# Moving four evictions to ScalarE, splitting the attention products and spreading the experts' rows, in a gated-delta-rule and mixture-of-experts kernel

## The reference

```python
x = L0_attn_hidden_states
xn = _layernorm(x, axis=-1)
x = x + _L0_attn_ref(xn, ...) + _L0_ffn_ref(xn, ...)

# _L0_attn_ref: gated delta rule, 16 key heads, 32 value heads (2 per key head), width 128
#   q, k, v, z = projections of xn; a causal convolution of 4 taps and silu over q, k, v
#   q, k normalised; beta = sigmoid(b); g = -exp(A_log) * softplus(a + dt_bias)
#   per chunk of tokens: T = inverse of (I - M), M strictly lower triangular from k k^T and decays
#   scan over the chunks, per head:
v_prime = k_cumdecay_i @ state
vn = v_i - v_prime
out = q_i * exp(g_i) @ state + attn @ vn
state = state * exp(g_last) + (k_i * exp(g_last - g_i)).T @ vn
#   then out * silu(z), an rms norm, and one product with W_out

# _L0_ffn_ref: attention with 16 heads, then 16 experts of which each token takes 4
#   (w1, silu gate, w2), plus a shared expert
routed = jnp.einsum('te,teh->th', wfull, down)
return hid + (routed + shared).reshape(b, s, h)
```

## Time and profile before

| | us |
|---|---|
| median of 3 runs | 1550.68 |
| lowest, highest | 1547.57, 1552.07 |
| the profiled execution's own time | 1548.47 |
| span of the profiled execution | 1546.7 |
| busy: TensorE / its weight loads | 1514.5 / 1069.7 |
| busy: VectorE / ScalarE / GpSimd | 1104.5 / 779.7 / 442.7 |

### The profile page before, as it was taken

The page is one execution under the profiler, slowest core; times in us unless marked ns, Lnnn a source line. Parts: engine busy times, 40 slices in busy tenths (PEclk is TensorE's granted clock), DMA queues, the critical chain, the costliest instruction groups (busy, mean ns, idle before and its releaser), DMA issues.

```text
span 1546.7 us, 29212 instructions
## 1 busy us (share of the span) xinstructions
PE 1514.5 (98%) x10946; PEld 1069.7 (69%) x10946; DVE 1104.5 (71%) x2452; ACT 779.7 (50%) x1680; POOL 442.7 (29%) x280
## 2 busy tenths in 40 slices
PE   6999999999999999999999999999999999999998
PEld 4666666767656776666767767767767668668667
DVE  5364544465366335698988988988888988988966
ACT  3444445344423334664564664664664565565552
POOL 1000000006024003354444444543442541541511
PEclk9999999999999999999999999999999999999999
DMA  4342433223144434324314414414313323223211
GB/s 135 99 150 96 156 124 109 66 64 125 54 128 130 124 109 120 94 51 97 100 35 107 107 32 108 105 36 106 78 50 91 70 60 86 69 66 86 60 22 35
DMA packets 225051, 136.88 MB, mean 89 GB/s; under 512 B 160976, under 2 KB 196304, under 8 KB 224912
## 3 DMA queue, kind: packets, MB, share of 16 engines
q1 hardware_dynamic: 221840, 126.62, 30.5%
q0 software_dynamic: 3072, 8.39, 1.8%
HBM read 94.85 MB, written 35.91 MB: 85 GB/s over the span
## 4 chain that ended last, share of the span: by engine, by line
PE 90%; DVE 3%; issue 2%; POOL 2%; ACT 1%; DMA 1%; SPq 0%; POOLq 0%; DVEq 0%; ACTq 0%
PE ps L953 7%; PE ps L814 7%; PE ps L575 7%; PE ps L835 6%; PE ps L670 5%; PE ps L600 4%; PE ps L1089 4%; PE ps L704 4%; PE ps L857 3%; PE ps L590 3%; PE ps L890 3%; PE ps L742 3%; PE ps L752 3%; PE ps L1112 3%; PE ps L867 3%; PE ps L889 2%
## 5 line engine op out<-in xcount | busy, mean ns | idle before, releaser
L1440 ACT ACTIVATE vs<-ps 128x256 f32<-128x256 f32 x128 | 49.2, 384 | 255.8 <-PE ps L857 251.6
L2389 POOL TENSOR_TENSOR qg<-qT,Ebc 128x1024 f32<-128x1024 f32 x32 | 74.7, 2354 | 354.4 <-PE ps L890 329.2
L1944 DVE SCALAR_TENSOR_TENSOR cv<-ps,cw,cv 128x1022 f32<-128x1022 f32 (+2 forms) x96 | 122.8, 1280 | 18.9 <-ACT cv L1380 14.9
L1955 DVE SCALAR_TENSOR_TENSOR cv<-ps,cw,cv 128x1022 f32<-128x1022 f32 (+2 forms) x96 | 122.6, 1277 | 4.0 <-ACT cv L1412 1.6
L835 PE MATMUL ps<-xnT,gz 128*128 128x512 f32 x256 | 121.0, 596 | 0.6 <-DVE cv L1944 0.6
L953 PE MATMUL ps<-wout,xT 128*128 128x256 f32 x480 | 120.2, 392 | 1.3 <-ACT vs L1427 0.9
L575 PE MATMUL ps<-xrT,cv 128*128 128x512 f32 x256 | 117.8, 593 | 1.1 <-ACT xrT L1277 0.8
L814 PE MATMUL ps<-xnT,gv 128*128 128x512 f32 x256 | 117.6, 603 | 0.5
L2083 DVE SCALAR_TENSOR_TENSOR total<-ps,rr,total 128x256 f32<-128x256 f32 x240 | 111.6, 481 | 5.7
L1340 ACT ACTIVATE we<-ps,bias 128x128 f32<-128x128 f32 (+3 forms) x128 | 65.8, 526 | 98.2 <-DVE bias L1764 98.2
L1760 DVE TENSOR_TENSOR ps<-ps,causal_neg 128x128 f32<-128x128 f32 x128 | 37.4, 292 | 105.2 <-PE ps L600 105.2
(11 more groups left out here) (265 smaller groups left out, 3567.9 us busy)
## 6 DMA issues: line engine op xcount, KB each, us to landing
xs_dram<-zeros SPq DMA_DIRECT2D x16, 1024.0 KB, 7.6
dec<-grow_dram SPq DMA_DIRECT2D x32, 512.0 KB, 4.7
Ebc<-erow_dram SPq DMA_DIRECT2D x32, 512.0 KB, 5.0
cv<-in_wqk SPq DMA_DIRECT2D x16, 512.0 KB, 3.6
xn<-xs_dram SPq DMA_DIRECT2D x47, 128.0 KB, 2.1
ys_dram<-yg SPq DMA_DIRECT2D x47, 128.0 KB, 2.0
we<-in_we SPq DMA_DIRECT2D x16, 352.0 KB
cv<-in_wv SPq DMA_DIRECT2D x16, 256.0 KB, 3.7
```

What stands on the lines that cost most here:

```text
L1944: ins = stt(row, pair(bank)[:, :, 0:S - k], cw[:, f, i, TAPS - 1 - k:TAPS - k], row, ALU.mult, ALU.add)
L1955: ins = stt(row, pair(bank)[:, :, 0:S - k], cw[:, n, 2 + r, TAPS - 1 - k:TAPS - k], row, ALU.mult, ALU.add)
```

## The change

- The copy of the first state of a head goes from VectorE to ScalarE (`first_states`), between `deltas(h, 0, b)` and `deltas(h, 1, b)`. The semaphore of the states is now counted up by both engines and is called `x_S`.
- ScalarE does all four evictions of the last merge: `beside_64(n, a)` and `blocks_of_128(n, a)`, a = 0, 1. VectorE's two are gone. In the lead-in `beside_64(0, 1)` stands ahead of `gate_silu(0, 1)`.
- `attention(n, 1)` stands behind `residuals(h, 1, b)` instead of ahead of the states.
- The experts' rows are added two tiles per head, in all 16 heads; GpSimd gathers a new group in every second head.

```diff
             def solved(h, m, b):
...
-                    pe.wait_ge(fl["a_p3"], h + 1)
-                    pe.wait_ge(fl["v_p3"], h + 1)
+                    pe.wait_ge(fl["a_p3"], 2 * h + 2)
...
             def second_of_128(n):
 
-                pe.wait_ge(fl["v_u3"], n + 1)
+                pe.wait_ge(fl["a_u3"], 2 * n + 2)
...
+            def first_states(h, b):
+                act.wait_ge(fl["p_w"], 6 * h + b + 1)
+                if h:
+                    act.wait_ge(fl["p_o"], 8 * h)
+                fn(St[:, 1, b * R:(b + 1) * R, :].rearrange("p r d -> p (r d)"), ps[:, b, R * D:],
+                   ACT.Copy).then_inc(fl["x_S"], 1)
...
-            def beside_64(n):
-                act.wait_ge(fl["p_u3"], 2 * n + 1)
-                fn(U3s[64:P, 0:8], ps[64:P, 0, :].rearrange("p (u c) -> p u c", u=8), ACT.Copy).then_inc(fl["a_u3"], 1)
+            def beside_64(n, a):
+                act.wait_ge(fl["p_u3"], 2 * n + a + 1)
+                fn(U3s[64:P, 8 * a:8 * a + 8], ps[64:P, a, :].rearrange("p (u c) -> p u c", u=8),
+                   ACT.Copy).then_inc(fl["a_u3"], 1)
...
             values(0, 0)
             values(0, 1)
-            beside_64(0)
+            beside_64(0, 0)
+            beside_64(0, 1)
             gate_silu(0, 1)
             decays(1, 0)
             decays(1, 1)
-            blocks_of_128(0)
+            blocks_of_128(0, 0)
+            blocks_of_128(0, 1)
...
                     for b in range(B):
                         deltas(h, 0, b)
+                    for b in range(B):
+                        first_states(h, b)
                     for b in range(B):
                         deltas(h, 1, b)
...
                 if ahead:
                     decays(f, 0)
                 if middle:
-                    beside_64(n)
+                    beside_64(n, 0)
                 if middle and not ahead:
                     last_values()
                 if ahead:
                     decays(f, 1)
                 if middle:
-                    blocks_of_128(n)
+                    beside_64(n, 1)
+                    blocks_of_128(n, 0)
+                    blocks_of_128(n, 1)
...
                 if middle:
                     system(n, 0)
-                if scan and middle:
-                    blocks_of_128(h)
                 if middle:
                     system(n, 1)
                 if scan and middle and h:
                     add_outputs(h - 1, 7, NT)
                 if middle:
-                    for r in range(R):
-                        attention(n, r)
+                    attention(n, 0)
                 if scan:
                     for b in range(B):
-                        states(h, 0, b)
+                        residuals(h, 1, b)
+                if middle:
+                    attention(n, 1)
                 if scan:
-                    for b in range(B):
-                        residuals(h, 1, b)
+                    add_experts(h // 2, h % 2)
                     if h == NK - 1:
+                        dve.wait_ge(sm["m_used"], 32)
                         add_outputs(h - 1, 6, NT)
-                    if h < 8:
-                        add_experts(h)
                     for b in range(B):
                         states(h, 1, b)
...
-                if 0 <= n < 8:
-                    expert_rows(n)
+                if h % 2 and n // 2 < 8:
+                    expert_rows(n // 2)
```

More of the change, by code:

```diff
@@ L284, in build @@
             "a_u1", "a_p1", "a_u2", "a_p2", "a_u3", "a_p3",
-            "v_ck", "v_cv", "v_ss", "v_k2", "v_cb", "v_M", "v_A", "v_R", "v_S", "v_g", "v_sxt", "v_sx", "v_add",
-            "v_base", "v_t0", "v_tt", "v_u3", "v_p3", "v_vs", "v_self",
+            "v_ck", "v_cv", "v_ss", "v_k2", "v_cb", "v_M", "v_A", "v_R", "x_S", "v_g", "v_sxt", "v_sx", "v_add",
+            "v_base", "v_t0", "v_tt", "v_vs", "v_self",
             "g_mask", "g_self", "g_cb", "g_qg", "g_eg", "g_wo", "g_rr", "g_nk", "g_zero",
@@ L840, in key_state @@
             def key_state(h, m, b):
-                pe.wait_ge(fl["v_S"], 6 * h + 2 * (m - 1) + b + 1)
+                pe.wait_ge(fl["x_S"], 6 * h + 2 * (m - 1) + b + 1)
                 mm(ps[:, b, 0:R * D], kT[:, h % 2, 4 * b + m, :], St[:, m % 2, b * R:(b + 1) * R, :],
@@ L1025, in second_beside_64_and_first_of_128 @@
             def second_beside_64_and_first_of_128(n):
-                pe.wait_ge(fl["a_u3"], n + 1)
+                pe.wait_ge(fl["a_u3"], 2 * n + 1)
                 if n == 0:
@@ L1499, in blocks_of_64, with blocks_of_128 @@
                    ACT.Copy).then_inc(fl["a_p2"], 1)
-            def beside_64(n):
-                act.wait_ge(fl["p_u3"], 2 * n + 1)
-                fn(U3s[64:P, 0:8], ps[64:P, 0, :].rearrange("p (u c) -> p u c", u=8), ACT.Copy).then_inc(fl["a_u3"], 1)
-            def blocks_of_128(n):
-                act.wait_ge(fl["p_p3"], 2 * n + 1)
-                fn(PT[0:64, 0:8, 64:P], ps[0:64, 0, :].rearrange("p (u c) -> p u c", u=8),
+            def beside_64(n, a):
+                act.wait_ge(fl["p_u3"], 2 * n + a + 1)
+                fn(U3s[64:P, 8 * a:8 * a + 8], ps[64:P, a, :].rearrange("p (u c) -> p u c", u=8),
+                   ACT.Copy).then_inc(fl["a_u3"], 1)
+            def blocks_of_128(n, a):
+                act.wait_ge(fl["p_p3"], 2 * n + a + 1)
+                fn(PT[0:64, 8 * a:8 * a + 8, 64:P], ps[0:64, a, :].rearrange("p (u c) -> p u c", u=8),
                    ACT.Copy).then_inc(fl["a_p3"], 1)
@@ L2010, in states @@
                 dve.wait_ge(fl["p_w"], 6 * h + 2 * m + b + 1)
[L2011 to L2020, removed]
-                    for r in range(R):
-                        last = stt(St[:, 1 - m % 2, b * R + r, :], St[:, m % 2, b * R + r, :], eg[:, h % 2, r, t:t + 1],
-                                   ps[:, b, (R + r) * D:(R + r + 1) * D], ALU.mult, ALU.add)
-                last.then_inc(fl["v_S"], 1)
+                dve.wait_ge(fl["g_eg"], h + 1)
+                dve.wait_ge(fl["p_o"], 8 * h + 2 * (m - 1) + b + 1)
+                dve.wait_ge(fl["x_S"], 6 * h + 2 * (m - 1) + b + 1)
+                for r in range(R):
+                    last = stt(St[:, 1 - m % 2, b * R + r, :], St[:, m % 2, b * R + r, :], eg[:, h % 2, r, t:t + 1],
+                               ps[:, b, (R + r) * D:(R + r + 1) * D], ALU.mult, ALU.add)
+                last.then_inc(fl["x_S"], 1)
             def gate(h, m, b):
@@ L2087, in add_outputs, with add_experts @@
                     ins.then_inc(fl["v_add"], 1)
-            def add_experts(i):
-                for a in range(4):
+            def add_experts(i, half):
+                for a in range(2 * half, 2 * half + 2):
                     t, j = i % 2 * 4 + a, i // 2
@@ L2131, in turned_beside @@
                 dve.transpose(T64c[BL:2 * BL, :, 0:BL], PT[0:BL, :, BL:2 * BL]).then_inc(fl["v_tt"], 1)
[L2133 to L2140, removed]
             scaled_rows(1)
@@ L2240, in _ @@
                 if middle:
-                    for r in range(R):
-                        attention(n, r)
-                if scan:
-                    for b in range(B):
-                        states(h, 0, b)
+                    attention(n, 0)
                 if scan:
@@ L2248, in _ @@
                         residuals(h, 1, b)
+                if middle:
+                    attention(n, 1)
+                if scan:
+                    add_experts(h // 2, h % 2)
                     if h == NK - 1:
+                        dve.wait_ge(sm["m_used"], 32)
                         add_outputs(h - 1, 6, NT)
-                    if h < 8:
-                        add_experts(h)
                     for b in range(B):
@@ L2379, in last_exponentials @@
                 if n >= 2:
-                    pool.wait_ge(fl["v_S"], 6 * (n - 1))
+                    pool.wait_ge(fl["x_S"], 6 * (n - 1))
                 pool.tensor_copy(eg[:, n % 2], Ebc[:, :, :, P - 1]).then_inc(fl["g_eg"], 1)
```

## The result

The changed kernel took 1553.16 us, the median of 20 runs (1551.39 to 1555.51), against 1550.91 for 20 runs of the kernel before (1547.26 to 1554.05). The ratio is 1.0018, 95% interval [1.0011, 1.0024]: slower by 2.8 us, between 1.7 and 3.7. The forecast was 1553.1. It was right in time, direction and main cause. That it came so near is in part luck: two things that it didn't have, one of each sign, nearly cancelled.

The account below looks back on a forecast made before the run. TensorE, busy 1514.5 of 1546.7 us, was taken as the bound. Lead-in 2.8, head 0 -0.5 and end 0.1 sum to +2.4, giving 1550.9 for the profiled execution and 1553.1 us as median; range 1549.5 to 1556.5.

Parts of the forecast that it names:

- The merge evictions in the loop: ScalarE doing all last-merge evictions: slack before TensorE asks for `PT` grows from 0.4 to 1.1 us; gain 0, cost 0.
- heads shorter than 58.9: Sign named in advance that would show the forecast wrong; it expected 58.95 us per head again in the loop.
- The first state: Loop, state copies on ScalarE ahead of `key_state`: 0.42 us each, slack 0.5 us, cost 0 and gain 0.
- the other way: Claim that the trace has VectorE faster by 0.05 us at 256-element copies, where the skill's estimates have ScalarE faster.
- The attention product behind the residuals: Loop, VectorE: `attention(n, 1)` ends at 1059.7, `turn_keys` needs it at 1060.27; slack 0.45 us, cost 0.
- Rival B: Loop's smallest slack used up: `turn_keys` finds `attention(n, 1)` late, 1557 to 1561 us with the lead-in; chance 0.14.
- The lead-in: Before the loop: `beside_64(0, 1)` delays silu 3.1 us, then scaling, `system(1, 1)` and `project_gates(1, 0, 0)`; TensorE loses 2.8 us.
- Rival A: The lead-in hides the delay, so the 2.8 us shrinks to nothing at best, 1550.3 us; chance 0.13.
- Head 0: Two additions instead of four follow the late gathers, so states slide less: -0.5 us, zero if gathers land 0.5 later.
- The end: Last head: `add_experts(7, 1)` ahead of the last `add_outputs` and `states` may delay `key_state`, 0 to 0.2 us, taken as 0.1.
- Rival C: Waits hidden in weight loads before `solved`, 0.29 us each, vanish: 1548.8 us with the lead-in, 1546.4 without; chance 0.06.

Follow-up runs that it names:

- e6: Kernel before with only the second eviction of `PT` (`blocks_of_128`) moved from VectorE to ScalarE; one execution, 1546.52 us beside 1547.62.
- e7: Kernel before with only the copy of the first states moved from VectorE to ScalarE; one execution, 1550.93 us.
- e3: Changed kernel with five extra matmuls, results unused, filling TensorE's wait ahead of `project_gates(1, 0, 0)`; 1553.06 us, 1.0026 against the kernel before.
- e8: Changed kernel with two extra matmuls, results unused, filling TensorE's wait ahead of `project_gates(1, 0, 0)`; 1550.34 us, 1.0008 against the kernel before.
- b0: Kernel before, unedited, executed once more for a second profile; head 0 took 58.96 us and the end 87.2.
- e5: Kernel before with only the experts' part: two additions per head, a gather every second head; one execution, 1547.09 us beside 1547.62.
- e2: Kernel before with only ScalarE's wait for the interleaved products put ahead of `gate_silu(0, 1)` in the lead-in; 1550.93 us, 1.0016.
- e10: Changed kernel with repaired lead-in, plus two extra products, results unused, ahead of the waiting `beside_32(15)` at the end; 1546.43 us, 0.9984 against the kernel before.
- e9: Changed kernel with lead-in repaired (`beside_64(0, 1)` moved behind the silu and two decays), second measurement; 1547.88 us, 0.9997 against the kernel before.
- e1: Changed kernel with lead-in repaired (`beside_64(0, 1)` moved behind the silu and two decays), first measurement; 1547.41 us, 0.9989 against the kernel before.

## Why the prediction was right, point by point

- *The merge evictions in the loop, "gain 0, since the old slack was positive already".* This step failed, and by one of the prediction's own signs, "heads shorter than 58.9": they are 58.89. I looked at who asks for the evicted tiles and not at what stood behind the eviction on VectorE: `system(n, 1)`, for which `project_gates` asked with nothing to spare. It ended at 1053.08 and TensorE's group, due at 1053.23, ran 0.07 long. Over the 13 stretches behind head 0 the loop went from 766.82 to 765.54 us, -1.3, and e6, whose 13 stretches take 765.6, puts all of that on this eviction.
- *The first state, cost 0 and gain 0.* Right; ScalarE's two copies take 0.83 as taken, and e7 brings no head to 58.89. The comparison of the engines beside it was misread. Of the kernel before, all copies of 128x256, ns of one (lowest, median, highest):

```profile
L2016 DVE COPY St<-ps x32: 412/415/425, 642.1 to 1519.4; 128x256 f32<-128x256 f32 x32
L1440 ACT ACTIVATE vs<-ps x128: 384/384/387, 639.5 to 1533.5; 128x256 f32<-128x256 f32 x128
```

  A pair lasts 0.74 us on VectorE and 0.83 on ScalarE because VectorE's second copy starts 0.33 us after the first, before that ends, while ScalarE's starts 0.45 after it, having waited for TensorE. One copy is 0.03 us faster on ScalarE, as the prediction's estimates of 0.36 and 0.39 have it; "the other way" is wrong.
- *The attention product behind the residuals, slack 0.45.* Right: it ends at 1062.85 and line 797 begins at 1063.44, its load 0.1 earlier. Rival B had no place.
- *The lead-in, 2.8.* Right within 0.05 us in the four links that lead to TensorE's wait: silu 633.84 (633.85), scaling 637.37 (637.4), `system` 641.16 (641.18), `project_gates` 642.53 (642.55). `solved(0, 0)` started at 639.28, 0.2 sooner than put, inside the 2.8. Rival A fell with that. What the step lacked is the clock: another 1.7 us behind the wait, which e3 and e8 take away by filling it.
- *Head 0, -0.5.* Right for the profile on which it rests, where it gave 0.6; b0 shows that this loss was not there in a second execution (58.96). In the changed kernel the two additions followed the attention product at 650.56 without a wait for the gathers. A term read from one profile behind a DMA's landing was a draw and should have been bounded at 0.
- *The end, 0 to 0.2.* The last head's `key_state` lost nothing. The end as a whole varied between 86.4 and 90.6 us over the fourteen profiles, whose ends are nearly the same, more than the whole effect of the change. It took 86.4 and 86.5 in the two where nothing was filled and the clock stayed at 1.00 (the first profile of before, and e5), 87.2 to 87.8 in the ten where it fell once, and 90.6 in e7. The forecast had no term for this.
- *Rival C*, hidden waits going, had the right thought and the wrong place and size: 0.07 per head at line 835, and not the 0.29 at `solved`.
- *Two slips without effect.* Head 13 has 14 instructions on GpSimd in the earlier trace rows, not 13; and C's time without the lead-in, 1546.4, leaves out the other two terms, -0.5 and 0.1, which make it 1546.0.

The sum that the runs give is 2.8 + 1.7 - 1.3 and 0 to -0.6 for head 0: +2.6 to +3.2, beside the measured 2.8 [1.7, 3.7]. The forecast's 2.4 is near it by luck, because 1.7 and -1.3 nearly cancel.

## What to carry to other kernels

Where one engine is busy all the time, cost a moved instruction by what stood behind it in its stream as much as by who reads its result; a hold-up of a few hundredths of a microsecond shows only as a group that runs long (1.95 for 1.88), so compare the start-to-start steps of equal groups. Moving an instruction with a late wait ahead of ready work in the short part before a loop can cost more than the loop gives in all its turns, and moving it back is one line. Compare two profiles only after a second profile of the same kernel: two terms of this study, 0.5 us in head 0 and 0.7 to 1.2 at the end, were draws.

## What the runs showed of the hardware that was not expected

After TensorE had been busy 1.16 of 3.5 us, its granted clock averaged 0.69 for 5.5 us, and the low clock cost 1.7 us behind 2.4 us of waiting. A wait of 1.7 us in e2 left it at 1.00. With the wait filled to 0.4 us (e8) or fully (e3) it stayed at 1.00, in e3 with a DMA share of 0.98 in the stretch behind. The same happens at the end in eleven of the fourteen profiles (the changed kernel: busy 1.53 of 4 us, then 0.66):

```profile
1504.00:1508.00 4.00, 1.53 (x66) 1.36 (x65) 2.82 (x4) 2.18 (x8) 0.07 (x1) 0.92 0.00 0
1508.00:1512.00 4.00, 4.00 (x56) 3.13 (x58) 3.89 (x5) 1.18 (x2) 0.00 (x0) 0.66 0.02 6
```

With that wait filled the runs spread over 0.8 us (e10), without it over 6.9 (e9). The clocks on record show that the longer executions are those with more of the low clock; where in them it fell is not shown, since only one execution of each kernel has a profile. Not all of the spread need lie at the end: head 0 starts between 631.33 (e3) and 634.44 us (e1) in the profiles, 3.1 us apart, although no edit changes what stands ahead of the lead-in.
